# A two-layer adaLN kernel: the convolution's first tap on ScalarE, group results head group first, gated sums in bank 7, some last reads on GpSimd, and new places

## What is computed

```python
h = layernorm(x) * (1 + ca) + sa          # layer 0
x = x + ga * attention(h)                 # 16 heads, 4 key groups, relative bias, softmax
h = layernorm(x) * (1 + cb) + sb
x = x + gb * moe(h)                       # 16 experts, silu, 4 of 16 routed in 2 of 4 groups
h = layernorm(x) * (1 + ca) + sa          # layer 1
x_inner, z = split(h @ W_in)              # selective scan
x_conv = silu(conv1d(x_inner, 4 taps) + conv_b)
dt, B, C = ...                            # from x_conv
state = scan(exp(dt * A), dt * B * x_conv)        # over time, 16 states for each of 256 channels
y = sum_n(state * C) * silu(z) + D_param * x_conv
x = x + ga * (y @ W_out)
h = layernorm(x) * (1 + cb) + sb
x = x + gb * tanh(h @ W1 @ W2 @ W3 + b)
```

## Time and profile before

| | |
|---|---|
| device time, 3 runs | 2369.48, 2375.01, 2380.74 us, median 2375.01 |
| the profiled execution | 2379.51 us, of which the span is 2377.7 |
| PE busy | 2021.9 us (85%) |
| DVE busy | 1844.5 us (78%) |
| ACT busy | 1618.9 us (68%) |
| POOL busy | 1602.3 us (67%) |
| granted TensorE clock, mean | 0.956 |

### The profile page before, as it was taken

How to read it: one execution, slowest core, us unless ns; L and a number is a source line. 1 busy time by engine, 2 the same in 40 slices (tenths; PEclk the granted TensorE clock), 3 DMA queues, 4 the chain that set the end, 5 groups by cost and what they waited for, 6 DMA issues and landing times. The chain is left out here.

```text
span 2377.7 us, 41007 instructions
## 1 busy us (share of the span) xinstructions
PE 2021.9 (85%) x11637; PEld 954.3 (40%) x11772; DVE 1844.5 (78%) x3195; ACT 1618.9 (68%) x4159; POOL 1602.3 (67%) x1369
## 2 busy tenths in 40 slices
PE   4779998989999999989899899989898998868443
PEld 2445444444444444444444444444444443323110
DVE  2544678787887878797888878887888877778986
ACT  3666767777777778677787778677777776544452
POOL 1011249696987869696977869696978868677653
PEclk9889999999999999999999999999999999989655
DMA  6645478777868787877868787777778686445451
GB/s 143 110 75 90 93 161 158 164 150 155 171 113 186 152 171 134 163 158 161 157 131 182 142 180 144 155 152 169 143 145 182 128 178 124 113 107 152 115 146 50
DMA packets 534922, 338.93 MB, mean 143 GB/s; under 512 B 353801, under 2 KB 453225, under 8 KB 534249
## 3 DMA queue, kind: packets, MB, share of 16 engines
q1 hardware_dynamic: 534700, 336.30, 68.8%
HBM read 242.36 MB, written 26.74 MB: 113 GB/s over the span
## 5 line engine op out<-in xcount | busy, mean ns | idle before, releaser
L1363 POOL TENSOR_TENSOR work<-work,bc 128x512 f32<-128x512 f32 x512 | 648.9, 1275 | 123.2 <-PE bank L1399 73.6
L1369 DVE TENSOR_TENSOR_SCAN work<-bank,work 128x512 f32<-128x512 f32 x512 | 621.4, 1214 | 127.1 <-ACT bank L1352 101.2
L1376 POOL TENSOR_TENSOR work<-work,bc 128x512 f32<-128x512 f32 x436 | 562.6, 1295 | 104.1 <-DVE work L1369 103.3
L1095 POOL TENSOR_TENSOR zh<-zh,w_bc 128x512 f32<-128x512 f32 x256 | 326.5, 1275 | 379.4 <-DVE zh L1088 372.6
L1352 ACT ACTIVATE bank<-work,neg_a 128x510 f32<-128x510 f32 x512 | 354.5, 693 | 252.8 <-DVE work L1369 235.4
L731 ACT ACTIVATE probs<-bank,nmax 128x256 f32<-128x256 f32 x1024 | 478.2, 481 | 23.9 <-DVE nmax L721 23.2
L721 DVE TENSOR_REDUCE nmax<-bank 128x2 f32<-128x512 f32 x512 | 333.3, 675 | 107.9 <-PE bank L713 107.9
L749 ACT ACTIVATE probs_t<-bank 128x512 f32<-128x512 f32 x512 | 307.3, 600 | 125.1 <-PE bank L775 88.9
L741 PEld LDWEIGHTS bank<-ident,probs 128*128 128x128 f32 x2048 | 250.8, 143 | 266.3 <-issue 193.6
L713 PE MATMUL bank<-ke,q_all 64*64 64x256 f32 x4096 | 288.3, 398 | 67.6 <-DVE zh L1088 47.1
L741 PE MATMUL bank<-ident,probs 128*128 128x128 f32 x2048 | 317.2, 278 | 17.0 <-ACT probs_t L749 16.0
(11 more groups left out here) (170 smaller groups left out, 2261.7 us busy)
## 6 DMA issues: line engine op xcount, KB each, us to landing
work<-dt_rows SPq DMA_DIRECT2D x256, 512.0 KB, 6.5
ke<-low SPq DMA_DIRECT2D x256, 256.0 KB, 5.4
w_bc<-w_rows_d SPq DMA_DIRECT2D x256, 256.0 KB, 5.5
q_all<-q_rows SPq DMA_DIRECT2D x1024, 8.0 KB
bc<-bc_rows SPq DMA_DIRECT2D x64, 256.0 KB, 9.5
x_in<-in_x SPq DMA_DIRECT2D x32, 256.0 KB, 4.8
dt_rows<-step SPq DMA_DIRECT2D x16, 512.0 KB, 3.0
dt_rows<-step SPq DMA_DIRECT2D x32, 256.0 KB, 6.4
```

The source lines that it names most:

```text
L1095: nc.gpsimd.tensor_tensor(zh[:, n % 3, :], zh[:, n % 3, :], w_bc[:, n % WB, :], ALU.mult).then_inc(m_p, 1)
L1363: nc.gpsimd.tensor_tensor(hb[at % HB], ring[n % RING][:, 1, :], bc[:, s, :], ALU.mult).then_inc(s_dbx, 1)
L1369: nc.vector.tensor_tensor_scan(hb[at % HB], decay_bank(p, m)[:, :], hb[at % HB], 0.0, ALU.mult, ALU.add).then_inc(s_h, 1)
L1376: nc.gpsimd.tensor_tensor(hb[at % HB], hb[at % HB], bc[:, SG + batch(m)[2], :], ALU.mult).then_inc(s_hc, 1)
```

## The change

It does five things. First, the first tap leaves DVE and becomes an ACT instruction with weight and bias as its scale and bias (`s_tap_scalar`, L1183 of the changed kernel). Second, group results are stored head group first: ACT copies bank 3 into `ao_raw` with a step in its read, the mask `mask_d` is laid out to match, and L839 (L834 before) reads both inputs in line and writes runs of eight. Third, `s_end_vector` writes its product into bank 7 in place of `z_gate`, its second half reads it there, and the next sum into bank 7 waits for the second half. Fourth, in the last two pairs the reads of batches with m % 4 = 1 go to POOL (8 for each pair). Fifth, nearly all places move, most of them by 1 to 4 steps.

```diff
         AT = dict(
-            a_out_tensor=[78, 143], a_out_scalar=[80, 143], s_end_vector=[447, 505],
+            a_out_tensor=[79, 143], a_out_scalar=[82, 146], s_end_vector=[446, 503],
...
-            nc.scalar.activation(ao_raw[:, :], bank[3][:, :], ACT.Copy).then_inc(a_ao, 1)
+            nc.scalar.activation(ao_raw[:, :].rearrange("p (i g t) -> p i g t", g=G, t=QB),
+                                 bank[3][:, :].rearrange("p (i t g) -> p i g t", g=G, t=QB), ACT.Copy).then_inc(a_ao, 1)
...
-            by_query = "p (t g) -> p t g"
-            nc.vector.tensor_tensor(ao[:, :, cols].rearrange("p g t -> p t g"), ao_raw[:, :].rearrange(by_query, g=G),
-                                    bank[3][:, :].rearrange(by_query, g=G), ALU.mult).then_inc(a_on, 1)
+            by_block = "p (i g t) -> p i g t"
+            nc.vector.tensor_tensor(ao[:, :, cols].rearrange("p g (i t) -> p i g t", t=QB), ao_raw[:, :].rearrange(by_block, g=G, t=QB),
+                                    bank[3][:, :].rearrange(by_block, g=G, t=QB), ALU.mult).then_inc(a_on, 1)
...
-            if back == 0:
-                dve.wait_ge(s_xz, 4 * p + h + 1)
...
-                nc.vector.tensor_scalar(a, x, conv_w[:, h, KC - 1:KC], conv_b[:, h:h + 1], ALU.mult, ALU.add).then_inc(s_cv, 1)
...
+            if back == 1:
+                dve.wait_ge(s_tap, 2 * p + h + 1)
             else:
...
+        def s_tap_scalar(act, p, h):
+            act.wait_ge(s_xz, 4 * p + h + 1)
+            if h:
+                act.wait_ge(s_xc, 2 * p + 1)
+            elif p:
+                act.wait_ge(dt_out[1], 32 * p)
+            nc.scalar.activation(conv_s, bank[4][:, :], ACT.Identity, bias=conv_b[:, h:h + 1],
+                                 scale=conv_w[:, h, KC - 1:KC]).then_inc(s_tap, 1)
...
+        def by_gpsimd(p, m):
+
+            return not copies(p, m) or (p >= FREE_PAIR and m % 4 == 1)
...
             if m == 3 and p:
-                pe.wait_ge(s_g, 2 * p)
+                pe.wait_ge(s_yv, 2 * p)
...
-            nc.vector.scalar_tensor_tensor(z_gate[:, h, :], z_gate[:, h, :], 0.5, bank[7][:, :], ALU.mult, ALU.mult).then_inc(s_g, 1)
+            nc.vector.scalar_tensor_tensor(bank[7][:, :], z_gate[:, h, :], 0.5, bank[7][:, :], ALU.mult, ALU.mult).then_inc(s_g, 1)
             dve.wait_ge(s_g, 2 * p + h + 1)
-            nc.vector.scalar_tensor_tensor(z_gate[:, h, :], x_conv(p, h), d_par[:, h:h + 1], z_gate[:, h, :],
+            nc.vector.scalar_tensor_tensor(z_gate[:, h, :], x_conv(p, h), d_par[:, h:h + 1], bank[7][:, :],
```

More of the change, by code:

```diff
@@ L253, in build @@
         b_y, b_back, b_x = sem("b_y"), sem("b_back"), sem("b_x")
-        s_xz, s_z, s_zg, s_cv, s_ct, s_xc, s_bc, s_bcc = (
-            sem("s_" + n) for n in ("xz", "z", "zg", "cv", "ct", "xc", "bc", "bcc"))
+        s_xz, s_z, s_zg, s_tap, s_cv, s_ct, s_xc, s_bc, s_bcc = (
+            sem("s_" + n) for n in ("xz", "z", "zg", "tap", "cv", "ct", "xc", "bc", "bcc"))
         s_dtp, s_dt, s_dtx_p, s_z0, s_z1, s_c, s_hd = (
@@ L307, in build @@
[L307 to L312, removed]
@@ new lines, in build @@
+            s_conv_vector=[[349, 351, 351], [358, 358, 361]], s_silu_vector=[355, 363],
+            s_zgate_vector=[390, 399], f_res_vector=511, f_stats_vector=512, f_end_vector=578,
+            head_scores_tensor=-6, head_max_vector=[0, 2], head_exp_scalar=[1, 4],
+            head_turn_tensor=[5, 9], head_turn_scalar=[6, 12], s_read_gpsimd=4, m_weigh_gpsimd=9,
+            s_input_gpsimd=-3, b_root_gpsimd=152, s_root_gpsimd=328, f_root_gpsimd=504,
+            s_step_vector=[369, 371], s_tap_scalar=[347, 356],
@@ L327, in build @@
[L327 to L332, removed]
@@ L1282, in s_rows_in_sync @@
                     sp.wait_ge(s_c, copies(p - 1, BATCHES - (5 if k == SG else 1)))
-                else:
+                if k >= SG and by_gpsimd(p - 1, BATCHES - (7 if k == SG else 3)):
                     sp.wait_ge(s_hc, reads(p - 1, BATCHES - (5 if k == SG else 1))[0])
@@ L1301, in copies @@
             return SG * (p - FREE_PAIR) + s + 2
+        def by_gpsimd(p, m):
+            return not copies(p, m) or (p >= FREE_PAIR and m % 4 == 1)
         def reads(p, m):
-            late = sum(1 for q in range(FREE_PAIR - 1, p + 1) for k in range(m + 1 if q == p else BATCHES) if copies(q, k))
+            late = sum(1 for q in range(FREE_PAIR - 1, p + 1) for k in range(m + 1 if q == p else BATCHES) if not by_gpsimd(q, k))
             return BATCHES * p + m + 1 - late, late
@@ L1702, in step_scalar @@
             for h in range(NH):
+                p = due("s_tap_scalar", st, h)
+                if p is not None:
+                    s_tap_scalar(act, p, h)
+            for h in range(NH):
                 p = due("s_conv_scalar", st, h)
@@ L1735, in step_vector @@
                 s_scan_vector(dve, *at)
-                if copies(*at):
+                if not by_gpsimd(*at):
                     s_read_vector(dve, *at)
@@ L1773, in step_vector @@
             for h in range(NH):
-                for k in range(KC):
+                for k in range(KC - 1):
                     p = due("s_conv_vector", st, h, k)
                     if p is not None:
-                        s_conv_vector(dve, p, h, k)
+                        s_conv_vector(dve, p, h, k + 1)
             for h in range(NH):
@@ L1805, in step_gpsimd @@
             at = batch_due("s_read_gpsimd", st)
-            if at is not None and not copies(*at):
+            if at is not None and by_gpsimd(*at):
                 s_read_gpsimd(pool, *at)
@@ L2024 @@
     ah = np.arange(P)
-    mask_d = ((ah[:, None] % H // (H // G) == np.arange(G * QB)[None, :] % G)
-              & (ah[:, None] // H == np.arange(G * QB)[None, :] // G)).astype(one)
+    mask_d = ((ah[:, None] % H // (H // G) == np.arange(G * QB)[None, :] // QB)
+              & (ah[:, None] // H == np.arange(G * QB)[None, :] % QB)).astype(one)
     sel_r = (ah[:, None] % (H // G) == np.arange(P)[None, :] // 32).astype(one)
```

168 lines of the change are left out of this document (87 added, 81 removed).

## The result

| | before | changed |
|---|---|---|
| median of the runs | 2376.54 us (4 runs) | 2403.02 us (4 runs, 2394.97 to 2405.91) |
| profiled execution / span | 2379.51 / 2377.7 us | 2405.91 / 2404.0 us |
| busy PE / DVE / ACT / POOL | 2021.9 / 1844.5 / 1618.9 / 1602.3 | 2036.0 / 1774.3 / 1643.3 / 1614.9 us |
| granted clock, mean | 0.956 | 0.947 |

The changed kernel is slower: ratio 1.0105, 95% interval 1.0086 to 1.0124. The forecast was 2351.5 us with a range of 2326 to 2380, so the sign was wrong. DVE got nearly the relief that was counted: 70 us less of busy time, for some 75 (4.1 us for each of 16 pairs, and 16 reads of 0.60). What it bought was less than what other pieces cost by being late.

A forecast was written before the change was run, and what follows sets the result against it. PE was taken as the steady bound, 121.1 us busy of a 132.30 us pair, and DVE in the last stage. 1.2 us over 14 pairs (17) plus tail 6 gave 23; from median 2375.0, less 23.5: 2351.5 us, range 2326 to 2380.

The forecast's parts named there:

- the term for the new places: Moved places in the steady pattern: +0.1 us a pair taken, between -1.3 and +1.3, most shifts adding no work.
- The price that was read: Weighing on POOL behind the root: 3.8 us later, less 1.0 slack, so PE waits 2.8 us at L1100.
- It costs at most 1.3 net: PE's 2.8 us stall at L1100 takes in later waits for ACT (0.87, 0.66), leaving at most 1.3.
- Both waits shrink: ACT's 1.57 us at L852 and DVE's 1.72 at a scan shrink, returning up to 1.3 a pair to DVE.
- 6 in the tail: Last two pairs: 3.4 us from pair 14 and 2.4 from pair 15, between 0 and 9.6.
- The routing's +0.4: PE's 1.49 us wait for L1088 at 1047.08: one L834 shorter by 0.37 ahead of it gives +0.4 a pair.
- the convolution: L1035's wait for the last tap: 0.80 us leaves DVE, ACT may hand back 0.3, so +0.5 a pair.
- the three other scalings: The other three L834, before L713's smaller waits for DVE: +0.2 us a pair in all.
- Cycle 7.1: Last pair's four batches: 7.41 us falls to about 7.07, bound by buffers; 0.35 x 7 = 2.4 us gained.
- (d): Rival: weighing behind the root stalls PE 2.8 us at L1100 each pair, nothing absorbs it; 2391 us, chance 0.13.
- The rule against the tap: Skill rule keeping plain multiply and add off ScalarE: the move loses on ACT what it gains, 2369 against 2351.5.

## Why the prediction was wrong

The kernels stand between before and changed as in this table. The middle columns are the profiled executions, a pair as the mean of eleven and the rest from the twelfth pair's z gate to the end.

| | a pair | the rest | ratio to before |
|---|---|---|---|
| before | 132.6 us | 574.8 us | 1 |
| all edits of the code at old places, second tap at 357 | 132.1 | 567.3 | 0.9949 |
| and the other new places | 132.8 | 560.3 | 0.9928 |
| and the late step and z places | 134.4 | 560.5 | 1.0020 |
| and the weighing at 9 and the early way back: the changed kernel | 136.2 | 558.5 | 1.0105 |

The last step but one is partly of the experiments' own making, since its wait for the z gate comes up only with the way out at its old place.

- **The step that failed** is the term for the new places, "+0.1 for the region, between -1.3 and +1.3", and the sentence that it rests on: "Most of them shift by 1 to 4 steps, with no work added. One has a price that I can read." A pair got 3.6 us longer and not 1.2 shorter, and it was moved instructions that did it. The price that was read, the root's, was put too low, the input that now stands ahead of the weighing was left out, and the step matmul's new place had a price that was put at nothing.
- **The weighing.** I priced the root ahead of it and not the input ahead of it. The stall at the root was right in size (3.13 for 2.8), and wrong in what it is worth. "It costs at most 1.3 net" is a pair's share; the root alone costs 28 to 30 us over the run, some 2 us a pair (the weighing at 9, with the roots ahead and with them behind). The waits behind did shrink, as said: 16.7 to 5.5 for ACT's exponents, 5.3 to none at L576. But PE's clock fell to half after some of the stalls, which takes back part of what is absorbed: 8.6 of 20.4 us over eleven pairs, by one execution of each of the two runs. The input ahead of the weighing costs another 18 us, and has its own mechanism, a wait of POOL for a DMA. That one could have been read in the kernel before, where POOL's timeline has the weighing ahead of the input that waits (2.63 us):

```profile
947.81 1.28 POOL L1095 TENSOR_TENSOR zh<-zh,w_bc 128x512 f32<-128x512 f32 x1 [0.23 <-DVE zh L1088]
951.71 1.27 POOL L1363 TENSOR_TENSOR work<-work,bc 128x512 f32<-128x512 f32 x1 [2.63 <-DMA work<-dt_rows]
```

- **The step matmul.** At 368 for 366 it keeps bank 4 from the next expert for 0.87 us in each pair, 11.3 us in 13 pairs of the changed kernel. It can be asked of an order beforehand: who needs the bank next, and does it stand directly behind? The z gate's tanh at 389 and 399 costs another 0.84 us a pair only where the output gate stands at 143. No run moved one of the two without the other, so what the step matmul costs by itself isn't shown beyond its wait.
- **The way out.** "Both waits shrink" came true: ACT's wait at L852, 12.6 us in eight pairs, is gone in the changed kernel, and DVE's for the decay went from 53.9 to 37.7 us (868 to 1926 us). That it gives back time isn't shown. What the prediction didn't see is that these places hang on others. The earlier normalization fits only a root that stands ahead of the weighing, and a root there stalls PE; the run with the weighing alone put back shows it.
- **The code.** Its term was mis-sized as well, though not in sign. Forecast were 1.1 us a pair and 6 in the tail, 23 in all with the +0.1; measured 12 with the tap well placed. A pair went from 132.6 to 132.1, so 0.5 and not 1.1. The routing's +0.4 is seen (the wait of 1.49 at 1047.08 became 1.10); the convolution gave 1.7 us in eight pairs (7.3 to 5.6), 0.2 and not 0.5; the three other scalings gave nothing that shows. Alone, the tap gave 7 us, layout and bank 7 together 9, and the reads 2. The sum of 18 is not told apart from the 12 of all together (interval 8 to 17).
- **The tail.** Cycle 7.1 forecast, 7.20 measured. The reads alone measured 2 us, too little to tell from 0 or from the 4 counted. The stretch behind the twelfth pair got 7.5 us shorter with the code alone, for 6 forecast, and another 7 with the other new places, most likely those of the last four pairs, which the prediction didn't price. These are single executions, but the five kernels here that have the new places of the last pairs lie within 558.5 to 562.6 us.
- **The sum.** The terms add up to 22.6, 23 was written and 23.5 taken off, which changes nothing here.
- **The rivals.** (d) had the sign and the first mechanism, at 0.13 and 2391. It missed the second wait for POOL and the step matmul. Its condition was met: in the changed kernel PE reached L1105 at 1033.0, and the weighing ended at 1036.1.
- **The rule against the tap.** The Trainium skill, page "ScalarE: Activation LUTs", section "Rules for kernel authors", would keep a multiply and add on VectorE. The tap alone measured 0.9970 (0.9957 to 0.9983) of before, so here the measurement decides against it. DVE is 10 us a pair busier than ACT, and the tap's place was free. The same page's section "What ACT_TABLE_LOAD costs" comes to about 0.80 us, an estimate, for such an activation; the trace has 0.777.
- **Bank 7.** The product's second half took 0.748 us beside a busy POOL, in all 32, against a median of 1.27 with both inputs in SBUF. This agrees with the port that VectorE with two SBUF inputs shares with GpSimd, which the Trainium skill names on its page "SBUF — State Buffer", section "Who interferes with whom".

What stays open: why the clock falls after some stalls and not after others of the same length, and which of the remaining new places take 0.7 us a pair (132.1 to 132.8) and which give the 7 us at the end. In the total the two cancel, as the intervals of 0.9949 and 0.9928 overlap. That the lower clock makes up part of the root's cost was read from the traces and not tested by itself.

## What to carry to other kernels

When a change moves instructions in in-order queues, price every move by what stands ahead of it in its new place and who waits behind it; here the durations of the moved instructions were foretold to 2%, and the sign of the whole was wrong. A short instruction that feeds the busiest engine belongs ahead of anything that waits for a DMA or for another engine, and two places that hand a result from one to the next are moved together or not at all. That holds for experiments too: twice here a place was put back without its partner, and the run made a wait of its own (2.67 us at L580, 0.84 at L1039). If a good edit of the code measures badly, try one place before giving up on it: the same edits lost 2.1% with the second tap at one place and gained 0.5% with it three steps earlier.

## What the runs showed that was not expected

- A PE stall of 3.14 us went over into 6.8 us at the 1.2 GHz level (clock 0.50 from 1582 to 1586, 1.00 from 1588 on), while the same stall at 1036 us left PE at 1.12 us for two L1105, full speed. PE was busy 125.87 us in that pair for the same instructions that took 121.40 in the one at 1013.
- DVE writing runs of eight f32 (L839) took 0.680 us, less than L824's wholly contiguous 0.691; single elements with a step took 1.057.
- The pattern of the changed kernel isn't steady. Pairs take from 132 to 140 us. Between the pair at 1013 and that at 1559, 5.6 us longer, 4.5 us are PE's busy time at the lower clock. PE's idle time grew by 1.1, while POOL's longest wait for its inputs' rows grew from 2.2 to 3.5 us.
